# Ternary feed-forward on one core: the middle tap of the depthwise convolution moves from TensorE to ScalarE, and the projections run two units ahead

## The reference, cut to what matters

```
def ffn(x, w1, conv_w, conv_b, w2):
    h = bit_linear(x, w1)                       # (8, 512, 1024)
    h = depthwise_conv1d(h, conv_w, conv_b)     # 3 taps along the 512 rows, padding 1
    h = silu(h)
    return bit_linear(h, w2)                    # (8, 512, 256)

def act_quant(x):                               # for every row
    scale = 127.0 / clip(max(abs(x), axis=-1), 1e-05)
    return clip(round(x * scale), -128, 127) / scale
```

## Time and profile before

| | |
|---|---|
| median of 3 runs | 3845.13 us (3836.37 to 3846.18) |
| the profiled execution, its own time | 3849.17 us |
| its span, first to last instruction | 3847.4 us |
| busy in the span | PE 3198.5 us (83%), DVE 2500.1 us (65%), ACT 2215.1 us (58%), POOL 1118.4 us (29%) |
| mean granted clock of TensorE | 0.912 of full speed |

### The profile page before, as it was taken

How to read it: one execution, slowest core, us unless ns; L and a number is a source line. 1 busy time by engine, 2 the same in 40 slices (tenths; PEclk the granted TensorE clock), 3 DMA queues, 4 the chain that set the end, 5 groups by cost and what they waited for, 6 DMA issues and landing times. The chain is left out here.

```text
span 3847.4 us, 67593 instructions
## 1 busy us (share of the span) xinstructions
PE 3198.5 (83%) x17361; PEld 1628.5 (42%) x17361; DVE 2500.1 (65%) x7668; ACT 2215.1 (58%) x2970; POOL 1118.4 (29%) x1194
## 2 busy tenths in 40 slices
PE   5999998899588888858987888888379999965997
PEld 3343332344333333225654555555134334325565
DVE  4777775777677677744225777878867777755431
ACT  1777777444188888962115666667537777750111
POOL 4344440000545555401104333321232211101332
PEclk8999999899799899988998999999589999985899
DMA  5322420000433333310018998997031221102232
GB/s 146 87 70 73 101 62 12 22 1 1 130 105 89 89 94 89 83 52 0 0 39 277 293 292 288 308 310 267 19 87 40 56 63 40 35 25 97 74 101 66
DMA packets 212153, 392.86 MB, mean 102 GB/s; under 512 B 24633, under 2 KB 76985, under 8 KB 211657
## 3 DMA queue, kind: packets, MB, share of 16 engines
q1 hardware_dynamic: 168777, 296.38, 27.8%
q10 hardware_dynamic: 36864, 83.90, 5.8%
q0 software_dynamic: 6144, 8.39, 1.3%
HBM read 189.88 MB, written 96.47 MB: 74 GB/s over the span
## 5 line engine op out<-in xcount | busy, mean ns | idle before, releaser
L460 DVE CUSTOM_DVE_ANT_0 A_sums<-A_p_ps,A_bias 128x512 bf16<-128x512 f32 x1536 | 1038.7, 687 | 434.5 <-PE A_p_ps L261 397.1
L529 ACT ACTIVATE A_probs<-A_p_ps 128x1024 f32<-128x1024 f32 x768 | 781.3, 1018 | 275.4 <-PE A_p_ps L276 184.9
L261 PE MATMUL A_p_ps<-A_k_stack,A_q_stack 96*128 96x512 bf16 x1536 | 603.0, 395 | 119.2 <-DVE A_nmax L460 110.3
L512 ACT ACTIVATE A_p_ps<-A_biasT 128x1024 f32<-128x1024 bf16 (+1 forms) x512 | 526.1, 1028 | 62.3 <-ACT A_probs L529 2.8
L276 PE MATMUL A_p_ps<-A_q_stack,A_k_stack 99*128 99x512 bf16 x1536 | 468.1, 386 | 41.3 <-ACT A_p_ps L512 36.6
L292 PE MATMUL A_oT_ps<-A_probs,A_v_aug 128*17 128x512 f32 x3072 | 417.5, 616 | 0.7 <-ACT A_probs L529 0.7
L261 PEld LDWEIGHTS A_p_ps<-A_k_stack,A_q_stack 96*128 96x128 bf16 x1536 | 149.4, 97 | 634.3 <-DVE A_nmax L460 541.5
L1100 DVE CUSTOM_DVE_ANT_0 A_scores<-A_qk_ps,A_rel_in 128x384 f32<-128x384 f32 (+3 forms) x512 | 232.4, 486 | 83.2 <-PE A_qk_ps L984 75.3
L1007 PE MATMUL A_t_ps<-ident,A_scores 128*128 128x128 f32 x1280 | 228.8, 301 | 58.2 <-DVE A_probsT L1090 49.9
L1090 DVE COPY A_probsT<-A_t_ps 128x384 f32<-128x384 f32 (+3 forms) x512 | 229.4, 485 | 55.7 <-PE A_t_ps L1007 48.2
L1155 ACT ACTIVATE A_rel_out<-A_rel_ps 128x1024 f32<-128x1024 f32 (+3 forms) x256 | 180.2, 704 | 144.8 <-PE A_rel_ps L973 143.5
(11 more groups left out here) (343 smaller groups left out, 5436.4 us busy)
## 6 DMA issues: line engine op xcount, KB each, us to landing
A_k_stack<-A_parts SPq DMA_DIRECT2D x192, 256.0 KB, 5.0
A_q_stack<-A_parts SPq DMA_DIRECT2D x192, 256.0 KB, 5.5
A_rel_dram<-A_rel_out ACTq DMA_DIRECT2D x64, 512.0 KB, 4.9
A_rel_in<-A_rel_dram SPq DMA_DIRECT2D x64, 512.0 KB, 5.3
A_rel_dram<-A_rel_out ACTq DMA_DIRECT2D x64, 384.0 KB, 4.8
A_rel_in<-A_rel_dram SPq DMA_DIRECT2D x64, 384.0 KB, 5.1
A_ctxT<-in_ctxT SPq DMA_DIRECT2D x32, 512.0 KB, 6.5
A_mask_in<-in_mask SPq DMA_DIRECT2D x64, 256.0 KB, 4.7
```

The lines of the kernel that those rows point to most:

```text
L261: nc.tensor.matmul(p1_ps[i % 2][:, :], q_stack[0:KS, a_par, j * GH + i, t * P:(t + 1) * P], k_stack[0:KS, a_par, j * GH + i, :], start=Tru ...
L460: nc.vector.tensor_tensor_reduce(out=sums[:, i % NX, :], in0=p1_ps[i % 2][:, :], in1=bias[:, t, :], scale=-1.0, scalar=3.4028235e38, op0=A ...
L512: nc.scalar.activation(p2_ps[half][:, :, :], turned, ACT.Copy).then_inc(seeded, 1)
L529: nc.scalar.activation(probs[:, s % 2 * 2 + half, :, :], p2_ps[half][:, :, :], ACT.Exp).then_inc(exp_done, 1)
```

## The change

- convolve keeps the outer taps only: two float32 matmuls instead of three, and they add to what the bank already holds (start=False).
- A new function seed on ACT writes the middle tap's product, hs times taps[c][1], into the bank cv_ps[c % 2]. It waits for h_scaled and for silu_done of two units before; convolve now waits for seed (seeded) in place of those two.
- Eight float32 matmuls of 128 columns ones x ones run once, before the frames, over both banks, so that the later matmuls add.
- project runs two units ahead instead of one. Once a batch, peaks and scales stay; rows_in moves from slot 6 to 4, on DVE normalise from 2 to 1, row_scales from 3 to 2, quantise_rows from 5 to 3, on ACT row_diag from 4 to 3 and rows_out from 6 to 4.
- tap_diag is 16 copies instead of 24.

```
+            for bank in cv_ps:
+                for t in range(TPB):
+                    last = nc.tensor.matmul(bank[:, t * P:(t + 1) * P], ones[:, :], ones[:, :], start=True, stop=True)
+            last.then_inc(bits_set, 1)
...
             def convolve(b, c):
                 if isinstance(b, int) and unit(b, c) == 0:
                     pe.wait_ge(tap_diags, 1)
-                pe.wait_ge(h_scaled, unit(b, c) + 1).then_inc(apart_pe, 1)
-                if not isinstance(b, int) or unit(b, c) >= 2:
-                    pe.wait_ge(silu_done, unit(b, c) - 1)
-                for k in range(3):
-                    last = nc.tensor.matmul(cv_ps[c % 2][:, :], tap_diag[:, c, k, :], hs[:, c % 2, k:k + S],
-                                            start=k == 0, stop=k == 2)
+                pe.wait_ge(seeded, unit(b, c) + 1)
+                for n, k in enumerate(OUTER):
+                    last = nc.tensor.matmul(cv_ps[c % 2][:, :], tap_diag[:, c, n, :], hs[:, c % 2, k:k + S],
+                                            start=False, stop=n == 1, skip_group_check=True)
                 last.then_inc(conv_done, 1)
...
             def frame(b, par, slots):
                 for c in slots:
-                    after = (b, par, c + 1) if c < HC - 1 else (b + 1, 1 - par, 0)
-                    if exists(after[0]) and c < HC - 1:
-                        project(*after)
+                    then = (b, par, c + 2) if c < HC - 2 else (b + 1, 1 - par, c + 2 - HC)
+                    if exists(then[0]):
+                        project(*then)
                     if exists(b):
                         convolve(b, c)
...
-                    if c == 6 and exists(b + 1):
+                    if c == 4 and exists(b + 1):
                         rows_in(b + 1)
-                    if c == HC - 1 and exists(after[0]):
-                        project(*after)
...
+            def seed(b, c):
+                if isinstance(b, int) and unit(b, c) == 0:
+                    act.wait_ge(bits_set, 1)
+                act.wait_ge(h_scaled, unit(b, c) + 1).then_inc(apart_act, 1)
+                if not isinstance(b, int) or unit(b, c) >= 2:
+                    act.wait_ge(silu_done, unit(b, c) - 1).then_inc(apart_act, 1)
+                nc.scalar.activation(cv_ps[c % 2][:, :], hs[:, c % 2, 1:S + 1], ACT.Copy, scale=taps[:, c, 1:2]).then_inc(seeded, 1)
...
             def frame(b, par, slots):
                 for c in slots:
+                    after = (b, c + 1) if c < HC - 1 else (b + 1, 0)
+                    if exists(after[0]):
+                        seed(*after)
                     if exists(b):
                         silu(b, par, c)
```

More of the change, by code:

```diff
@@ L1386, in ffn_bitnet @@
     RING = 4
+    OUTER = (0, 2)
     ctx = ExitStack()
@@ L1403, in ffn_bitnet @@
         taps, conv_bias = sb("taps", [P, HC, 3], F32), sb("conv_bias", [P, HC], F32)
-        tap_diag = sb("tap_diag", [P, HC, 3, P], F32)
+        tap_diag = sb("tap_diag", [P, HC, len(OUTER), P], F32)
         stats, moments, rstd, minus_half = norm_buffers(sb)
@@ L1435, in ffn_bitnet @@
         size_done = sem("size_done")
+        bits_set, seeded = sem("bits_set"), sem("seeded")
         peak_turned, sc_step, sc2_ready, diag2_ready = (sem(n) for n in ("peak_turned", "sc_step", "sc2_ready", "diag2_ready"))
@@ L1690, in frame @@
                         quantise(bq, pq, cq)
-                    if exists(after[0]) and (c == HC - 1 or exists(b)):
+                    if exists(after[0]):
                         scale(*after)
@@ L1706, in frame @@
                             stats_of(b + 1)
+                        if c == 1:
+                            normalise(b + 1)
                         if c == 2:
-                            normalise(b + 1)
+                            row_scales(b + 1)
                         if c == 3:
-                            row_scales(b + 1)
-                        if c == 5:
                             quantise_rows(b + 1)
@@ L1751, in _ @@
             for c in range(HC):
-                for k in range(3):
-                    last = nc.scalar.activation(tap_diag[:, c, k, :], ident[:, :], ACT.Copy, scale=taps[:, c, k:k + 1])
+                for n, k in enumerate(OUTER):
+                    last = nc.scalar.activation(tap_diag[:, c, n, :], ident[:, :], ACT.Copy, scale=taps[:, c, k:k + 1])
             last.then_inc(tap_diags, 1)
@@ L1763, in frame @@
                         batch_scale(b - 1, 1 - par)
-                    if c == 4 and exists(b + 1) and exists(b):
+                    if c == 3 and exists(b + 1) and exists(b):
                         row_diag(b + 1)
-                    if c == 6 and exists(b + 1):
+                    if c == 4 and exists(b + 1):
                         rows_out(b + 1, 1 - par)
```

## The result

| | before | after |
|---|---|---|
| median | 3845.26 us (3836.37 to 3846.18, 4 runs) | 3809.31 us (3805.36 to 3814.43, 4 runs) |
| ratio, with its 95% interval | | 0.9913 (0.9898 to 0.9929) |
| the profiled execution, its own time | 3849.17 us | 3814.43 us |

The account below looks back on a forecast made before the run. PE was taken to bound the slots, plus one wait for DVE's output rows. Gains 2.3 + 2.6 + 4.8 + 26.5 - 6.8 + 3.7 = 33 us gave 3816 profiled, 3812 as median; range 3802 to 3832.

Parts of the forecast that it names:

- The bound: PE bounds the slots before; losing a tap saves 0.86 us a unit, PE's frame 30.6 to 23.7, below DVE's 26.2.
- The seed: On ACT, 0.70 us a unit between DVE's scale and PE's convolution, hidden by projecting two units ahead.
- its sign of being wrong: PE's wait for the seeds: over 0.3 us a unit would show the prediction wrong.
- The walk: A full frame followed from PE's slot 0: DVE's output rows done at 20.4, frame 28.8 us at full clock.
- a sign of being wrong: The frame's heavy slots: taking over 4.5 us would show the prediction wrong.
- The clock: Lower-clock stretch on PE about the wait before slot 5, 1.7 us in four of five frames, 6.8 lost.
- rival 2: PE's clock falls for most of heavy slots 0 to 4: 25 us slower, 3865; chance 0.06.
- The small terms: Gains at the stage's start 2.3 us, frame 0 2.6, frame 1 4.8, last frame 3.7; ones matmuls just hidden.
- Rival 3: Another wait, as DVE's fold for Abs or the batch scales, takes back 4 to 5 us a frame: 3840 to 3850; chance 0.06.
- Rival 4: No lower clock in the stage and more overlap than walked: gain 40 to 45 us, 3803; chance 0.10.

Follow-up runs that it names:

- e4: Changed kernel with DVE's output rows in slot 4 moved ahead of the rounding and the fold; 3797.10 us, ratio 0.9875.
- e8: e6 with frames 2 to 5 written out instead of looped and batch 1's rows kept in frame 0; 3795.36 us, ratio 0.9870.
- e2: Changed kernel put back to the old order, keeping the seed on ACT and two taps on PE; 3821.86 us, ratio 0.9940.
- e3: Changed kernel with each seed written by four activations of 128 columns instead of one of 512; 3811.53 us, ratio 0.9916.
- e7: Changed kernel with sixteen ones x ones matmuls at the start instead of eight; 3810.56 us, one run.
- e1: Changed kernel with three taps on PE again, no seed and no ones matmuls, keeping the new order; 3835.27 us, ratio 0.9982.
- e12: Same kernel as e10 (changed kernel, frames 2 to 5 written out), timed again; 3803.44 us, ratio 0.9895.
- e10: Changed kernel with frames 2 to 5 written out instead of looped, no other edit; 3800.15 us, one run.
- e5: Changed kernel with DVE's statistics, normalise and row scales of batch b+2 moved to slots 5, 6 and 7; 3799.26 us, ratio 0.9894.
- e6: e5's spread of row work and e4's earlier output rows together, on the changed kernel; 3798.71 us, ratio 0.9895.
- e9: e6 with batch 1's statistics kept in frame 0, the loop kept, and row_scales moved to slot 0 of the next frame; 3796.88 us, ratio 0.9886.

## Why the prediction was right

- **The bound.** PE loses 0.86 a unit and the frame then belongs to DVE up to slot 4: right. e4 takes 0.94 us out of the wait behind it and the frame gets 0.94 shorter; e8 relieves DVE's heavy slots and the frame falls to 26.8, of which DVE is busy 26.1.
- **The seed.** 0.70 was taken, 0.685 measured. That the new order hides it is shown by e2 (19.0 us of waits for seeds in the old order, 3.6 in the new) and e3 (0.5 dearer in each unit costs 0.54 a frame). The 3.6 us are 0.06 a unit, far under the 0.3 that the prediction named as its sign of being wrong.
- **The walk.** 28.8 forecast, 29.09 measured. Counted as there, from PE's slot 0 (it ends slot 7 at 772.15 + 0.43 = 772.58, so it began at 743.49): output rows done at 20.6 for 20.4, the contraction begun and done 0.69 later for 0.63, slots 5 to 7 in 7.76 for 7.7. Each step holds within 0.25, and slots 0 to 4 took 4.3 us each in the mean (743.49 to 764.82), under the 4.5 named as a sign of being wrong.
- **The clock.** Four of five frames at 1.7 were forecast; four came, frames 3 to 6, at 1.2 to 2.0 above frame 2. In sum 6.4 against 6.8. With them three of the five frames last longer than the 30.5 us that the prediction gave as their upper end. That it was four is luck: the prediction gave no ground for the number, the same order had five in e7, and its ground for the fall, "about this wait led to the lower level", was too simple. e1 waits 1.67 to 1.93 us in frames 2 to 5 and none falls; e12 has equal waits and one in five; in e3 the fall came behind two waits of under 1 us and not behind this one. In e4, with 0.90 us, there was none. Before the change three of the five frames had it, so that the clock took much the same from both kernels (5.9 us before, against the mean of the other two frames, and 6.4 after). The Trainium skill ("TensorE: Matmul & The Clock Gate", section "Why this matters for your kernels") advises against long idle gaps between bursts of matmuls. e4 agrees in direction; but the falls here came behind waits shorter than those that the page warns of, the longest 2.40 us in the kernel before and 1.84 in the changed one, while e2 kept its full clock behind 3.40 and 3.32 us in frames 5 and 6. So the page did not foretell rival 2, as the prediction read it, and the length of a gap alone does not decide. Rival 2, by which most heavy slots would run at the lower level, is refuted by the frames' means of 0.94 to 1.00.
- **The small terms.** Start 3.0 for 2.3, frame 0 2.0 for 2.6, frame 1 4.7 for 4.8, the end 4.3 for 3.7; e7 shows that the ones matmuls are covered with little or nothing to spare.
- **Rival 3** did not come. DVE does wait where it said, 14.8 us in the stage for Abs and 7.7 for the batch scales, but in frame 2 its waits for Abs, 1.55 us, all lie behind slot 4, where PE leads, and its wait for the batch scales is 0.47 us, where the walk had 0.4. **Rival 4** needed a full clock and less waiting; the changed kernel had neither. e4, a further edit, had both.

What the loop costs can be seen in part. Some handovers between engines come later in it: in frames 2 to 5 of the changed kernel each Abs starts 0.87 to 0.90 us behind its Silu, in all its other frames 0.79 to 0.82, and in e10 and e12 0.78 to 0.82 in every frame, but for one Abs each. A seed starts 0.98 behind its scale for 0.90 unrolled (slot 3 of frame 2), the contraction of slot 4 0.26 behind the end of the output rows for 0.10; the projection behind its scale, 0.83, does not differ. In each pair of rows the first is Silu, the second Abs, outside the loop and in it:

```profile
697.81 0.69 ACT L1731 ACTIVATE B_act_out<-B_cv_ps,B_conv_bias 128x512 f32<-128x512 f32 x1
698.62 0.63 ACT L1735 ACTIVATE B_sizes<-B_act_out 128x512 f32<-128x512 f32 x1
...
749.77 0.67 ACT L1731 ACTIVATE B_act_out<-B_cv_ps,B_conv_bias 128x512 f32<-128x512 f32 x1
750.64 0.63 ACT L1735 ACTIVATE B_sizes<-B_act_out 128x512 f32<-128x512 f32 x1 [0.20 <-ACT B_act_out L1731]
```

In e10 against the changed kernel DVE's output rows start 0.25 us earlier in frame 2 (16.49 for 16.74 us into it), PE's contraction behind them another 0.17, and the statistics of the next frame 0.19 more. Still open is why these handovers are slower in the loop, and what brings the lower clock behind one wait and not behind another. Nor was e4 tried unrolled.

## What to carry to other kernels

When work leaves the busiest engine, walk one period through the queues: the gain stopped where DVE's once-a-batch work and one wait for its last piece took over, and moving that piece up two places (12 us) brought a third of what the whole change had. A product moved to a third engine lengthens the way between two others, so move the producer one unit further ahead with it: with the old order, 19 us of waits for the seed were left (the moves of the once-a-batch work went with it and were not tried apart). And look at whether a loop is worth its price: writing out four frames gave 9 us for no other edit, about 2.4 of them the shorter frames themselves and 5 the clock in the executions profiled.

## What was not expected

- At the back edge of a loop DVE stood still for 2.8 to 3.0 us with nothing late (e5, e6, e9). It is not seen where DVE waits for others in the slots before the edge (the changed kernel, e4), nor unrolled (e8); its cause is open.
- The same frame takes 29.07 to 29.09 us in the loop and 28.48 written out, at full clock both times.
- With waits of 1.83 to 1.92 us the granted clock fell in 13 of 15 frames of three executions with the loop and in 1 of 10 of two without; with 1.67 to 1.93 us in e1, also with the loop, in none of four. In e2, with waits of 3.3 to 3.65 us, it fell in three frames and stayed up in two. In e3 it fell behind waits of 0.93 and 0.85 us.
- A Copy of 128x512 float32 with a scale from SBUF into a bank takes 0.685 us; four of 128 columns take 0.5 us more in all.
